# A Mamba and mixture-of-experts block on one core: every engine's order of steps worked out anew, with tables of their own for the first two and the last two slots

## The chip, the core and the metric

The kernel runs on one core of a Trainium2 chip. A core has five instruction queues that run side by side, each strictly in its own order: TensorE (PE), VectorE (DVE), ScalarE (ACT), GpSimd (POOL) and SyncE (SP, which here only issues DMAs). They meet at semaphores alone. The metric is the device time of one launch, in microseconds; the median of the runs is what counts.

## What is computed

The reference is one adaLN block on x of 8 batches x 1024 tokens x 256 channels, float32:

```
h = layernorm(x) * (1 + ca) + sa
x = x + ga * mamba(h)          # rmsnorm, in_proj (512+512), causal conv of 4 taps, silu,
                               # x_proj -> dt, B, C; delta = softplus(...)
                               # s = s * exp(delta * A) + delta * B * u   (16 states x 512 channels, over 1024 tokens)
                               # y = sum over states of s * C, + u * D, * silu(z), out_proj, + h
h = layernorm(x) * (1 + cb) + sb
x = x + gb * ffn(h)            # sigmoid gate, top 4 of 16 experts, each silu(h @ w) * (h @ v) @ out, + a shared expert
```

The six modulation vectors (sa, ca, ga, sb, cb, gb) come from silu(c) @ wmod, one set for each batch.

## The kernel before

The 8192 tokens are cut into 16 chunks of 512. The program is a software pipeline of 18 slots. In slot t three stages run side by side on three chunks: **prepare** of chunk t (norms, in_proj, conv, x_proj, delta, du), **scan** of chunk t-1, and **mix** of chunk t-2 (z gate, out_proj, second norm, router, experts, store). So slot 0 holds only prepare, slot 1 prepare and scan, slots 2 to 15 all three, slot 16 scan and mix, slot 17 mix alone.

Scan is the backbone. A slot has 16 states s and for each 4 channel groups b, 64 groups in all. For each (s, b): POOL makes `scaled` (L713: db_sb = du * B), ACT makes `exp` (L957: da_ps = exp(delta * A)), DVE runs `scan` (L1196, a tensor_tensor_scan over 512 tokens). da_ps has two buffers (NDA = 2), so `exp` number n waits for scan n-2; db_sb has five. When the four scans of a state are done, PE transposes the states into rows_ps (`rows`, L1416, four of them, j = 0 to 3, into two buffers), ACT weighs each with C (`c_scale`, L930) or DVE adds it onto the one before (`c_join`, L1238, states 1, 5, 9, 13; `y_join`, L1247, state 15), and a DMA issued on POOL accumulates it into y_sb (`c_add`, L725). `carry` (L921) keeps the last column for the next chunk.

Mix runs 36 expert units u in a slot, 18 for each half chunk. A unit is `expert_in` (PE, L1480, 24 matmuls into one of three shared PSUM banks), `e_tanh` (ACT, L1023), `e_act` and `e_mul` (DVE, L1296 and L1302; the last frees the bank), `e_weigh` (POOL, L756, with a row that SP loads by `w_load`, L599), and `expert_out` (PE, L1498, 4 matmuls into moe_ps). act has three buffers: `e_tanh` of u waits for `expert_out` of u-3.

Other steps that are named below: `xd`, `xd_t` (PE, L1376, L1383), `dt_high`, `xd_evac` (ACT, L877, L884), `dt_low`, `xd_t_evac` (DVE, L1158, L1164), `dtp` (PE, L1393), `dt_bias` (ACT, L891), `soft_exp` (ACT, L903 and L905), `delta` (DVE, L1170); `x_norm` (ACT, L796), `x_scale`, `x_shift` (DVE, L1122, L1131), `hn_high`, `hn_low` (L823, L1175), `xi` (PE, L1364); at the start of the program `fold` (DVE, L1072 to L1084), `in_low` (DVE, L1054), `mod_rows` (DVE, L1090 to L1105); in slots 1 and 2 `ein_low` (DVE, L1319, nine of them, which split the expert weights).

The order in which each engine takes its steps is not written out by hand. `schedule` gives every step a place in time: a base value from the step lists (`scan_steps`, `prepare_steps`, `mix_steps`, `start_steps`), plus SLOT for each slot, plus a correction by kind of step (SHIFT), by kind and index (PLACE), and for slot 0 (FIRST), slot 17 (LAST) and the program's start (START). Steps are sorted by that value, each engine walks the sorted list and emits the steps that are its own, and the same list gives out the three PSUM banks. The number sets only the order: no engine waits for a time.

## Time and profile before

| | |
|---|---|
| median of 3 runs | 2739.45 us (2736.83 to 2739.89) |
| span of the profiled execution, first to last instruction | 2736.3 us |
| what lies around the span (median less span) | 3.15 us |
| busy: DVE, PE, POOL, ACT | 2398.1, 2351.9, 2256.4, 1945.8 us |
| share of the span: DVE, PE, POOL, ACT | 88%, 86%, 82%, 71% |
| mean granted TensorE clock | 0.943 |

The profiled execution's span and the median are of different executions, 3.15 us apart. Busy shares are means over stages of different kinds; a slot has to be looked at by itself, which is why the rows further down begin with a table by slot. An engine's idle time is listed with what ended it. "x4" in a timeline row is four like instructions in one run. Start and end times are microseconds from the span's start.

### The profile page before, as it was taken

The page shows a single profiled execution, that of the slowest core. Times are in us where ns is not written, and L with a number is a line of the kernel's source. Part 1 is how long each engine was busy: PE and PEld are TensorE (multiplying, and loading weights), DVE is VectorE, ACT ScalarE, POOL GpSimd, SP SyncE. Part 2 cuts the span into 40 slices and gives each one's busy share as a digit, 9 for nine tenths or more (in the row PEclk, how much of TensorE's full clock was granted, in tenths as well). Part 3 has the DMA queues.
Part 4 walks back from the last instruction along what each step waited for, and adds up shares of the span by engine and source line. Part 5 has one row for each costly group of instructions (what it writes and reads, how often), then busy time and mean ns, then how long its engine had stood idle before and what let it go on. Part 6 is the DMA issues. An engine that isn't in the chain of part 4 may idle for free.

```text
span 2736.3 us, 51736 instructions
## 1 busy us (share of the span) xinstructions
PE 2351.9 (86%) x16084; PEld 1889.2 (69%) x16084; DVE 2398.1 (88%) x3815; ACT 1945.8 (71%) x3713; POOL 2256.4 (82%) x2222
## 2 busy tenths in 40 slices
...
GB/s 80 164 143 108 146 148 137 162 115 154 121 145 156 137 161 113 151 130 148 147 132 168 120 145 121 155 156 122 163 114 153 130 159 147 117 156 134 155 70 55
DMA packets 131520, 372.07 MB, mean 136 GB/s; under 512 B 19720, under 2 KB 22408, under 8 KB 130992
## 3 DMA queue, kind: packets, MB, share of 16 engines
...
q8 instruction: 131, 2.15, 0.3%
...
## 4 chain that ended last, share of the span: by engine, by line
POOL 30%; issue 22%; PE 20%; DVE 13%; ACT 7%; DMA 2%; POOLq 1%; DVEq 0%; ACTq 0%; SPq 0%
POOL db_sb L713 16%; PE bank_ps L1480 7%; DVE states L1196 5%; PE moe_ps L1498 5%; POOL act L756 4%; PE rows_ps L1416 4%; POOL y_sb L725 3%; POOL y_sb L734 2%; ACT da_ps L957 2%; PE bank_ps L1376 2%; ACT c_rows L930 1%; POOL du_sb L700 1%; DMA w_sb<-w_dram 1%; DVE act L1296 1%; DVE bank_ps L1143 1%
## 5 line engine op out<-in xcount | busy, mean ns | idle before, releaser
L713 POOL TENSOR_TENSOR db_sb<-du_sb,b_sb 128x512 f32<-128x512 f32 x1024 | 1473.6, 1655 | 32.8 <-DVE states L1196 32.2
L957 ACT ACTIVATE da_ps<-delta,a_sb 128x512 f32<-128x512 f32 x1024 | 696.6, 689 | 170.4 <-DVE states L1196 168.2
L1416 PE MATMUL rows_ps<-ident,states 128*128 128x128 f32 x4096 | 611.4, 287 | 120.9 <-DVE states L1196 85.2
L1480 PE MATMUL bank_ps<-h2T_high,ein_w_high 128*128 128x256 f16 x2304 | 633.9, 275 | 83.8 <-DVE act L1302 50.0
L1196 DVE TENSOR_TENSOR_SCAN states<-da_ps,carry,db_sb 128x512 f32<-128x512 f32 x512 | 644.9, 1273 | 19.0 <-ACT da_ps L957 17.6
L1416 PEld LDWEIGHTS rows_ps<-ident,states 128*128 128x128 f32 x4096 | 503.3, 148 | 210.6 <-DVE states L1196 98.0
L1196 DVE TENSOR_TENSOR_SCAN states<-da_ps,db_sb 128x512 f32<-128x512 f32 x512 | 613.9, 1213 | 34.5 <-ACT da_ps L957 26.3
L1480 PE MATMUL bank_ps<-h2T_low,ein_w_high 128*128 128x256 f16 x2304 | 634.0, 275 | 0.0
L1480 PE MATMUL bank_ps<-h2T_high,ein_w_low 128*128 128x256 f16 x2304 | 633.6, 275 | 0.0
L1498 PE MATMUL moe_ps<-eout_sb,act 128*128 128x256 f32 x2304 | 583.3, 387 | 41.5 <-POOL act L756 40.7
L756 POOL TENSOR_TENSOR act<-act,w_sb 128x256 f32<-128x256 f32 x512 | 472.9, 1115 | 164.0 <-DVE act L1302 141.7
L725 POOL DMA_DIRECT2D y_sb<-c_rows x352 | 379.6, 1078 | 179.1 <-ACT c_rows L930 105.5
L930 ACT ACTIVATE c_rows<-rows_ps,xd_sb 128x512 f32<-128x512 f32 x704 | 467.9, 682 | 70.6 <-PE rows_ps L1416 66.2
L1498 PEld LDWEIGHTS moe_ps<-eout_sb,act 128*128 128x128 f32 x2304 | 408.6, 191 | 113.6 <-POOL act L756 68.8
L1023 ACT ACTIVATE act<-bank_ps 128x256 f32<-128x256 f32 x576 | 218.5, 382 | 286.2 <-PE moe_ps L1498 144.8
L1296 DVE SCALAR_TENSOR_TENSOR act<-act,bank_ps 128x256 f32<-128x256 f32 x576 | 231.6, 407 | 146.0 <-ACT act L1023 145.7
L1480 PEld LDWEIGHTS bank_ps<-h2T_high,ein_w_high 128*128 128x128 f16 x2304 | 226.9, 98 | 127.2 <-DVE act L1302 58.0
L1480 PEld LDWEIGHTS bank_ps<-h2T_high,ein_w_low 128*128 128x128 f16 x2304 | 227.2, 99 | 38.4
L1480 PEld LDWEIGHTS bank_ps<-h2T_low,ein_w_high 128*128 128x128 f16 x2304 | 227.3, 99 | 28.1
L1302 DVE TENSOR_TENSOR act<-act,bank_ps 128x256 f32<-128x256 f32 x576 | 225.2, 410 | 3.3
L1238 DVE SCALAR_TENSOR_TENSOR c_rows<-rows_ps,xd_sb,c_rows 128x512 f32<-128x512 f32 x256 | 181.5, 740 | 3.3 <-PE rows_ps L1416 2.5
L1143 DVE SCALAR_TENSOR_TENSOR bank_ps<-xi_pad,convw_sb,bank_ps 128x512 f32<-128x512 f32 x192 | 143.4, 748 | 5.1 <-ACT bank_ps L858 3.6
...
## 6 DMA issues: line engine op xcount, KB each, us to landing
...
b_sb<-b_dram SPq DMA_DIRECT2D x128, 512.0 KB, 4.8
w_sb<-w_dram SPq DMA_DIRECT2D x256, 256.0 KB, 3.5
...
```

The lines of the kernel that those rows point to most:

```text
L713: pool.tensor_tensor(db_sb[:, n % NDB, :], du_sb[:, slots[t][0][0], b, :], b_sb[:, k % NBPAIR, s % BPAIR, :], ALU.mult).then_inc(sem["scal ...
L725: pool.dma_start(y_sb[:, slots[t][0][0], CPAIR * pair:CPAIR * pair + CPAIR, :], c_rows[:, n % NCR, :, :], accum_op=ALU.add).then_inc(c_add ...
L756: pool.tensor_tensor(place, place, w_sb[:, k % NWROWS, n % WROWS, :], ALU.mult).then_inc(sem["e_weighed"], 1)
L930: ac.activation(c_rows[:, n % NCR, j % CPAIR, :], rows_ps[j % 2][:, :], ACT.Copy, scale=xd_sb[:, slots[t][0][0], j, s:s + 1]).then_inc(sem ...
L957: ac.activation(da_ps[n % NDA][:, :], delta[:, slots[t][0][0], b, :], ACT.Exp, scale=a_sb[:, b, s:s + 1]).then_inc(sem["exp_done"], 1)
L1023: ac.activation(act[:, u % 3, :], bank(key)[:, 0:HALF], ACT.Tanh, scale=0.5 / LIFT).then_inc(sem["e_tanhed"], 1)
L1196: v.tensor_tensor_scan(states[:, n % (2 * NB), :], da_ps[n % NDA][:, :], db_sb[:, n % NDB, :], first, ALU.mult, ALU.add).then_inc(sem["sca ...
L1296: v.scalar_tensor_tensor(place, place, 1.0, bank(key)[:, 0:HALF], ALU.add, ALU.mult).then_inc(sem["e_acted"], 1)
L1302: v.tensor_tensor(place, place, bank(key)[:, HALF:CH], ALU.mult).then_inc(bank_read(key)[0], 1)
L1416: last = pe.transpose(rows_ps[j % 2][:, b * P:b * P + P], states[:, step % 2 * NB + b, j * P:j * P + P], ident[:, :])
L1480: last = pe.matmul(bank(key)[:, a * HALF:a * HALF + HALF], ein_w16[w][:, k, e // 2, at:at + HID], h2T[h][:, k, q * HALF:q * HALF + HALF], ...
L1498: last = pe.matmul(moe_ps[:, n, :], act[:, u % 3, n * P:n * P + P], eout_sb[:, e, :], start=first and n == 0, stop=u % NALL == NALL - 1, s ...
```

## The change

All tables of corrections have new values, and two more tables stand beside FIRST and LAST: SECOND for slot 1 and NEAR_LAST for slot 16. SHIFT and PLACE now also reach the steps of the program's start and the loads of the expert weights (`early_loads`), which had none or other corrections before. Every step that was there is still there, with the same operands, buffers and transfers. Four waits are added, so that `xd_t_evac` may stand later than it did.

```
+def early_loads():
+    out = [(SLOT - 2, ("eout_load",)), (SLOT + 20, ("eout_fold",))]
...
+    ends = {0: FIRST, 1: SECOND, last - 1: NEAR_LAST, last: LAST}
+    listed = [(at - LEAD_P0, START.get(what[0], 0.0), 0.0, 0.0, what) for at, what in start_steps()]
...
-            at = round(at + SLOT * t + SHIFT.get(what[0], 0.0) + PLACE.get(place(what), 0.0) + ends.get(what[0], 0.0), 5)
...
+        listed += [(at + SLOT * t, SHIFT.get(what[0], 0.0), PLACE.get(place(what), 0.0), ends.get(t, {}).get(what[0], 0.0), what) for at, what in mine]
+    latest, keyed = {}, []
+    for n, (at, shift, own, end, what) in enumerate(listed):
+        at = at + shift + own + end
+        latest[what[0]] = max(at, latest.get(what[0], at))
+        keyed.append((latest[what[0]], n, what))
+    order = [what for _, _, what in sorted(keyed)]
...
                         ac.wait_ge(sem["rows_full"], NJ * step + j + 1)
+                        if s == 0 and j == 0:
+                            ac.wait_ge(*bank_read(("xd_t", t - 1)))
...
                     def xd_t_evac(t):
                         key = ("xd_t", t)
+                        if nS(t):
+                            v.wait_ge(*c_scales(NS * nS(t) - 2, NJ - 1))
...
+                        if s == JOINED[0] and j == 0:
+                            v.wait_ge(*bank_read(("xd_t", t - 1)))
...
+                        if not JOINED and j == 0:
+                            v.wait_ge(*bank_read(("xd_t", t - 1)))
```

What the new values come to, sorted: of 3392 steps on DVE 2380 stand at another place in its queue, of 3566 on ACT 2804, of 2690 on PE 1814, of 2099 on POOL 1381, of 523 on SP 309; the mean move is 1 to 2.3 places. The order is the same in each of the slots 2 to 15. Parts of it, with the steps that follow each scan, exp or rows group (s,b or s,j) before and after:

```
                before                                             after
DVE scan 6,2    dt_low, c_join 5.2, 5.3                            c_join 5.2
    scan 6,3    xd_t_evac                                          c_join 5.3, dt_low, e_act 9, e_mul 9
    scan 7,3    e_act 12, e_mul 11, 12                             e_act 12, e_mul 12, e_act 13, e_mul 13
    scan 8,0    e_act 13, e_mul 13                                 -
    scan 8,1    e_act 14                                           xd_t_evac
    scan 8,2    e_mul 14                                           -
    scan 8,3    -                                                  e_act 14, e_mul 14
    scan 12,0   e_act 24, 25, e_mul 24, 25                         -
    scan 12,1   -                                                  e_act 24, e_mul 24
    scan 12,2   e_act 26                                           -
    scan 12,3   e_mul 26                                           e_act 25, 26, e_mul 25
    scan 13,0   e_act 27, 28                                       e_mul 26, e_act 27
    scan 13,1   e_mul 27, 28                                       -
    scan 13,2   -                                                  e_act 28
    scan 13,3   e_act 29, 30, e_mul 29, 30                         e_mul 27, 28
ACT exp 6,3     dt_high, xd_evac                                   carry 5, e_tanh 9      (dt_high after exp 6,2)
    exp 7,0     e_tanh 9, 10                                       xd_evac
    exp 8,1     c_scale 7.0, e_tanh 13, dt_bias 0                  e_tanh 13, dt_bias 0, carry 7, c_scale 7.0, 7.1, dt_bias 1
    exp 8,2     c_scale 7.1, dt_bias 1, 2, e_tanh 14               dt_bias 2
    exp 8,3     c_scale 7.2, dt_bias 3, e_tanh 15, c_scale 7.3     e_tanh 14, c_scale 7.2, dt_bias 3
    exp 9,0     soft_exp 0, carry 8, e_tanh 16                     c_scale 7.3
    exp 9,1     c_scale 8.0                                        e_tanh 15, carry 8, soft_exp 0, e_tanh 16, c_scale 8.0, 8.1
PE  rows 11,3   expert_in 27, 28                                   expert_in 27, expert_out 24
    rows 12,0   expert_out 24, 25                                  -
    rows 12,1   expert_in 29                                       expert_in 28, expert_out 25
```

In all eleven states that ACT weighs, `c_scale` j = 0 and j = 1 now stand in a row ahead of the exp of the next state's group b = 2; before, j = 1 stood behind it. In the program's start, on DVE: before `x_scale 0, x_shift 0, fold, x_scale 1, norm_lift, x_shift 1, mod0_gate, hn_low 0, 1, in_low 0, 1, mod_rows, tap ...`; after `mod0_gate, norm_lift, x_scale 0, x_shift 0, x_scale 1, x_shift 1, in_low 0, 1, fold, hn_low 0, 1, tap ... u 3, mod_rows`. At the start of slot 1 ACT has before `x_norm 0, exp 0,0, x_norm 1`, after `x_norm 0, x_norm 1, exp 0,0`. Slot 1 has its nine `ein_low` at other places among the scans, and `skip_t` moved from states 9 to 11 to states 12 and 13. In slot 17 the engines keep their kinds of steps in the same sequence, with `e_act` and `e_mul` of one unit more often side by side; `z` of j = 0 and 1 on PE stand ahead of rows 14,2.

## Rows read from the trace of the kernel before

**Rows 1.** Busy time by slot: start:end length, each engine's busy us (instructions), granted clock, DMA.

```profile
0.00:79.50 79.50, 31.51 (x84) 12.40 (x84) 36.82 (x79) 41.68 (x81) 23.28 (x34) 0.72 0.33 119
79.50:234.80 155.30, 82.62 (x342) 55.04 (x342) 130.52 (x132) 110.15 (x195) 115.87 (x101) 0.63 0.60 140
234.80:395.70 160.90, 143.76 (x1002) 116.26 (x1003) 149.08 (x238) 119.87 (x225) 139.97 (x139) 0.97 0.59 137
...
716.60:876.20 159.60, 144.03 (x1006) 116.74 (x1006) 145.48 (x237) 120.92 (x237) 140.75 (x139) 0.97 0.60 139
...
2478.20:2616.50 138.30, 124.02 (x898) 105.42 (x895) 123.97 (x191) 86.89 (x158) 119.41 (x118) 0.96 0.62 143
2616.50:2736.30 119.80, 102.03 (x709) 84.36 (x708) 49.08 (x126) 24.61 (x56) 31.93 (x43) 0.96 0.18 53
```

**Rows 2.** Waits of DVE, 486 to 1770 us (eight slots): total us, times, longest.

```profile
DVE act L1296 <- ACT act L1023: 51.5, 60, 1.7
...
DVE dt L1158 <- ACT th_p L884: 8.7, 8, 1.1
```

**Rows 3.** Timeline of DVE, slot 5: start, us, what [idle before <-releaser].

```profile
782.59 0.68 DVE L1158 TENSOR_TENSOR dt<-bank_ps,dt 16x512 f16<-16x512 f32 x1 [1.11 <-ACT th_p L884]
...
795.36 0.42 DVE L1296 SCALAR_TENSOR_TENSOR act<-act,bank_ps 128x256 f32<-128x256 f32 x1 [0.77 <-ACT act L1023]
798.91 0.42 DVE L1296 SCALAR_TENSOR_TENSOR act<-act,bank_ps 128x256 f32<-128x256 f32 x1 [1.54 <-ACT act L1023]
...
804.56 0.42 DVE L1296 SCALAR_TENSOR_TENSOR act<-act,bank_ps 128x256 f32<-128x256 f32 x1 [0.90 <-ACT act L1023]
...
809.82 1.22 DVE L1196 TENSOR_TENSOR_SCAN states<-da_ps,db_sb 128x512 f32<-128x512 f32 x1 [0.92 <-ACT da_ps L957]
...
836.69 0.42 DVE L1296 SCALAR_TENSOR_TENSOR act<-act,bank_ps 128x256 f32<-128x256 f32 x1 [0.60 <-ACT act L1023]
837.98 1.22 DVE L1196 TENSOR_TENSOR_SCAN states<-da_ps,db_sb 128x512 f32<-128x512 f32 x1 [0.87 <-ACT da_ps L957]
...
842.42 0.42 DVE L1296 SCALAR_TENSOR_TENSOR act<-act,bank_ps 128x256 f32<-128x256 f32 x1 [1.23 <-ACT act L1023]
...
849.07 0.42 DVE L1296 SCALAR_TENSOR_TENSOR act<-act,bank_ps 128x256 f32<-128x256 f32 x1 [0.97 <-ACT act L1023]
```

**Rows 4.** Timeline of ACT, slot 5, ahead of three of these waits.

```profile
781.89 0.59 ACT L884 ACTIVATE th_p<-bank_ps 48x512 f32<-48x512 f32 x1
...
797.34 1.27 ACT L891 ACTIVATE delta<-bank_ps,dtb_sb 128x512 f32<-128x512 f32 x2 [0.24 <-PE bank_ps L1393]
798.50 0.38 ACT L1023 ACTIVATE act<-bank_ps 128x256 f32<-128x256 f32 x1
...
842.00 0.38 ACT L1023 ACTIVATE act<-bank_ps 128x256 f32<-128x256 f32 x1 [0.68 <-PE moe_ps L1498]
```

**Rows 5.** Timeline of the start, slots 0 and 1: DVE and PE.

```profile
14.75 0.69 DVE L1131 TENSOR_TENSOR u_sb<-bank_ps,mod_p 128x512 f32<-128x512 f32 x1
...
17.65 0.69 DVE L1122 TENSOR_TENSOR bank_ps<-bank_ps,mod_p 128x512 f32<-128x512 f32 x1
...
29.25 2.47 DVE L1054 SCALAR_TENSOR_TENSOR in_w_low<-states,norm_sb,in_w_high 128x1024 f16<-128x1024 f32 x2
...
31.82 0.59 PE L1364 MATMUL bank_ps<-hnT_high,in_w_high 128*128 128x512 f16 x1 [3.85 <-DVE in_w_low L1054]
...
78.15 0.70 DVE L1122 TENSOR_TENSOR bank_ps<-bank_ps,mod_p 128x512 f32<-128x512 f32 x1 [1.55 <-ACT bank_ps L796]
```

**Rows 6.** Line L1319 (`ein_low`): duration ns min/median/max, first and last start.

```profile
L1319 DVE SCALAR_TENSOR_TENSOR ein_w_low<-zg,ein_w_high x4: 1529/2198/4226, 96.0 to 190.7; 128x1024 f16<-128x1024 f32 x4
```

**Rows 7.** Waits of ACT over the same eight slots.

```profile
ACT c_rows L930 <- PE rows_ps L1416: 33.3, 56, 2.8
```

**Rows 8.** The chain of waits in order of time: start, us, what.

```profile
301.56 2.62 PE bank_ps L1480 x24
```

**Rows 9.** The page's costliest groups: instructions | busy us, mean ns | idle before.

```profile
L957 ACT ACTIVATE da_ps<-delta,a_sb 128x512 f32<-128x512 f32 x1024 | 696.6, 689 | 170.4 <-DVE states L1196 168.2
```

More of the change, by code:

```diff
@@ L238 @@
-FIRST = {"b_store": -4.638, "delta": -2.819, "dt_bias": 2.771, "dt_high": 2.569, "dt_low": 6.847, "dtp": -4.658, "du": 20.092,
-         "ein_high": -18.513, "ein_load": -0.56, "ein_low": 2.016, "h_rms": -0.524, "h_scale": -5.721, "h_square": -2.549,
-         "hn_high": -0.965, "hn_low": -3.241, "hn_t": -7.947, "in_high": 23.347, "in_low": -6.337, "r_add": 5.286, "r_gate": 2.226,
-         "r_store": 3.856, "skip": 5.238, "skip_evac": 9.562, "skip_t": 8.304, "soft_exp": 7.839, "soft_ln": 4.557, "tap": 0.054,
-         "u": 3.728, "u_tanh": 1.139, "x_load": 5.378, "x_norm": -2.74, "x_rstd": -14.374, "x_scale": 3.508, "x_shift": 4.515,
-         "x_stat": -7.043, "xd": 0.786, "xd_evac": -0.005, "xd_t": 13.73, "xd_t_evac": 11.585, "xi": -6.047, "xi_center": -0.781,
-         "xi_copy": -1.708}
@@ L250 @@
-START = {"a_made": -8.949, "constants": -7.533, "ct_silu": -16.404, "ct_tanh": -13.749, "first_loads": 27.458, "fold": 1.055,
-         "in_high": 0.627, "in_low": 7.261, "mod0": 3.212, "mod0_gate": 3.313, "mod0_rows": -4.136, "mod_rows": 0.914, "mod_store": 18.312,
-         "mods": -12.286, "norm_lift": 17.868, "out_scale": 1.297}
+SHIFT = {"b_load": -4.075, "b_store": -0.774, "c_add": 1.548, "c_join": 0.51, "c_scale": 0.671, "carry": 1.751, "delta": -1.404,
+         "dt_bias": 0.716, "dt_high": -1.074, "dt_low": 6.436, "dtp": -1.259, "du": -3.209, "e_act": -0.057, "e_mul": -0.129,
+         "e_tanh": -0.303, "e_weigh": 1.236, "ein_high": -2.54, "ein_load": -8.035, "ein_low": 3.444, "eout_fold": 7.161,
+         "eout_load": -39.417, "exp": 1.131, "expert_in": -0.101, "expert_out": 0.782, "h2_high": 0.138, "h2_low": -0.01, "h2_scale": 0.42,
+         "h2_t": -2.304, "h_rms": -4.436, "h_scale": -3.293, "h_square": 0.94, "hn_high": -0.686, "hn_low": 0.906, "hn_t": 3.499,
+         "logit": -1.011, "logit_exp": 2.301, "mod_m_load": -7.536, "mod_p_load": -51.943, "op": 1.293, "op_gate": 1.514, "out_add": 1.84,
+         "out_gate": 0.676, "out_store": 3.191, "r_add": 11.77, "r_gate": 1.021, "r_load": 12.711, "r_store": -3.854, "router": 3.104,
+         "rows": 0.174, "scaled": 1.14, "scan": 0.004, "skip": -0.464, "skip_evac": 4.69, "skip_t": -1.302, "soft_exp": -3.082,
+         "soft_ln": 1.864, "tap": 0.19, "u": -0.176, "u_tanh": 0.428, "w_evac": -1.906, "w_load": -0.429, "w_store": 7.456, "w_t": -3.769,
+         "x1": 1.091, "x1_norm": -4.802, "x1_rstd": -5.323, "x1_stat": 1.485, "x_load": -7.339, "x_norm": 0.681, "x_rstd": 5.697,
+         "x_scale": -0.157, "x_shift": -0.7, "x_stat": -1.105, "xd": -4.991, "xd_evac": 3.144, "xd_t": 6.368, "xd_t_evac": 8.145,
+         "xi": -1.404, "xi_center": -0.012, "xi_copy": -0.284, "y_evac": -1.028, "y_gate": -0.757, "y_join": 0.428, "y_t": -0.212,
+         "z": -5.131, "z_gate": -0.023, "z_tanh": -2.943}
```

85 lines of the change are left out of this document (44 added, 41 removed), and 144 rows, old and new, of the table PLACE.

## The prediction

> **What bounds the kernel now.** I read the table of busy time by slot first [rows 1]. Slots 2 to 15 are alike: 160.2 us each on average (234.8 to 2478.2 is 14 slots), of which DVE is busy 145.5 to 149.1, PE 143.8 to 144.0, POOL 140.0 to 140.8 and ACT 119.9 to 120.9. So the kernel is bound by DVE with PE and POOL close behind, and yet some 13 us of each such slot are DVE's idle time. No engine can go below its busy time by a change of order, and all operations are kept; the idle time is the whole of what the change can win, 14 x 13 = 182 us at the very most in those slots. The two ends are looser: slot 0 has 36.8 us of DVE in 79.5, slot 1 has 130.5 in 155.3, slot 16 124.0 (and PE 124.0) in 138.3, slot 17 102.0 of PE in 119.8.
>
> Second, who ends DVE's idle time: in eight slots, 51.5 us before `e_act` waiting for `e_tanh`, 8.7 us before `dt_low` waiting for `xd_evac` [rows 2]; the reader is to see that ACT ends it, though ACT is the least busy of the four. Third, where in the slot: the timeline of slot 5 [rows 3]. The waits come in three places, the same in every slot. Place A, states 6: 1.11 us before `dt_low`. Place B, states 8 and 9: 0.77 (`e_act` 13), 1.54 (`e_act` 14), 0.90 (`e_act` 15), 0.92 (a scan), 4.1 us. Place C, states 12 and 13: 0.60, 0.87, 1.23, 0.97, 3.7 us. Together 8.9 of the 13 us. Between them DVE runs nearly without a gap.
>
> **Part 1, the inner slots.** Place A: `xd_evac` runs at 781.89 and ends at 782.48, and `dt_low` starts at 782.59 [rows 3, 4], because ACT reaches it only after the two `dt_high` while DVE has nothing between scan 6,2 and `dt_low` to fill the time. After, DVE puts `c_join` 5.2, scan 6,3 and `c_join` 5.3 in between, 1.22 for the scan and about 0.69 for each `c_join`, as for the other 512-column steps of DVE, 2.6 us of work [rows 3, 5]; ACT has an exp, an `e_tanh` and one more exp in there, 0.69 + 0.38 + 0.69 = 1.8 us [rows 4, 9]. The wait goes: 1.1 us. Place B: `e_tanh` 14 starts at 798.50 behind `c_scale` and two `dt_bias` that alone take 797.34 to 798.61 [rows 4]; DVE wants it one scan after `e_act` 13. After, `e_act` 14 stands behind scan 8,3, two scans later (2.4 us against a wait of 1.54), so that wait goes. But `e_act` 13 now stands right behind scan 7,3, while its `e_tanh` still follows an exp that needs that scan: I keep some 0.6 of its 0.77. And the two `soft_exp` (two ACT instructions over 1024 columns each; an estimate of 2.1 us from exp's 0.69 for 512 columns) still sit among exps in state 9; going through ACT's queue from scan 7,3 to scan 10,0 I find 0.6 + 0.4 + 0.7 + 0.7 + 0.5 = 2.9 us of waits where 4.1 were. Gain 1.2. Place C: `e_tanh` 27 starts at 842.00 when PE ends `expert_out` 24 [rows 4], which stands on PE behind `expert_in` 28, a run of 2.62 us [rows 8]. After, `expert_out` 24 stands ahead of `expert_in` 28, so it comes up to 2.62 us sooner, and on DVE `e_act` 28 has two scans more to wait. The 0.60 + 1.23 + 0.97 (2.8 us) of `e_act` waits should shrink to next to nothing; the scan's 0.87 I leave.
>
> Sum: 1.1 + 1.2 + 2.8 = 5.1 us a slot, if nothing is given back. Something will be: PE and POOL have only 16 and 20 us of idle time a slot [rows 1], and every wait that goes on DVE pulls the next scan, and with it rows, `c_scale` and `c_add`, forward into engines that are as full. I take half, 2.6 us a slot; the bounds are 0 (all given back) and 5.1. 14 slots x 2.6 = 36 us.
>
> **Part 2, the four waits.** `xd_t_evac` now waits for the `c_scale` of state 14 of the slot before, which was over seven states ago; `c_scale` 0.0 and `c_join` 1.0 wait for an `xd_t_evac` of the slot before, half a slot ago. Behind each are queued the rest of ACT's or DVE's steps, but all three are fulfilled when they are reached. The fourth is never emitted. Some three waits a slot that are met at once: between 0 and 0.1 us each, an estimate from `dt_low`'s start 0.11 after the end of what it waits for [rows 3, 4]; 3 x 16 x 0.1, 5 us in all at most. I take 0.
>
> **Part 3, slot 0.** Before, DVE does `fold` between `x_shift` 0 (ends 15.44) and `x_scale` 1 (starts 17.65) [rows 5]; the first thing that waits for `x_shift` 1 is the squaring on ACT. After, `fold` stands behind `in_low`: 17.65 - 15.44 = 2.2 us sooner, of which I take 2.0, since `x_norm` 1 has to be there. Then `in_low`, 2.47 us at 29.25, is the last that `xi` on PE waits for (31.82) [rows 5]. After, it stands ahead of `hn_low`, in a stretch where DVE waits anyway: 2.4 us more. `mod_rows` moves off the path too, into the wait for dt. At the start of slot 1 `x_norm` 1 no longer stands behind a table load and an exp; its `x_scale` starts at 78.15 after a wait of 1.55 [rows 5], of which 1.4 go, for the first exp then comes last. Sum 5.8 us; 3 to 7. SP's big expert load is put ahead of the loads of x and B there; I take it as hidden behind `du` and `x_rstd` on POOL, and let the bounds of this part stand for up to 3 us if it is not.
>
> **Part 4, slot 1, slot 16 and the tail.** Slot 1 has 24.8 us of DVE idle time and TensorE at 0.63 of its clock, near the lower of its two levels (1.2 GHz) [rows 1]; the order there is so different that I can't follow it step by step. Its nine `ein_low` are the same instruction and last between 1.5 and 4.2 us in the four that one row shows [rows 6], so what they cost depends on when they come. With a least duration of 1.5 and a median of 2.2, nine of them carry some 6 us that another order could win or double: bounds -6 to +6 for the slot, I take a gain of 2. The Trainium skill (SBUF — State Buffer, "SBUF: two separate sides") has a rule for this: VectorE and GpSimd share one port pair, and a VectorE instruction with two SBUF inputs and a GpSimd instruction that reads SBUF shut each other out for a whole instruction. The spread of the row agrees; by that rule `ein_low` ought to stand where POOL is idle, and the new order gives no sign that it does, so by the page the gain of slot 1 would be 0 and the sum 2 us smaller. For slot 16 and 17 I take 2 us: PE, which carries the tail, is idle 14.3 + 17.8 us there [rows 1], most of it in the one chain from y to the router weights, whose steps have the same sequence as before. Bounds 0 and 8.
>
> **Sum.** 36 + 5.8 + 2 + 2 = 46 us. The profiled execution has a span of 2736.3 and the median is 3.15 more; taken off the median, 2739.45 - 46 = 2693.
>
> **The rivals.** (1) *Given back in full* (0.13): the inner slots are set by a ring of DVE, ACT, PE and POOL and a wait that goes comes back elsewhere; only the start is won. 2739.45 - 5.8 - 2 = 2731. For it: three engines are within 7 us of one another [rows 1]. Against it: the waits are DVE's own, and DVE is the fullest. (2) *More than half* (0.15): nothing is given back, and slot 1 and the tail give more. 14 x 5.1 + 7 + 6 + 8 = 92, so 2647, or 2660 where a little is lost. (3) *Slower: the paired c_scale* (0.15). In eleven states `c_scale` j = 1 now stands ahead of the exp that scan b = 2 waits for. ACT stands still there if PE has not yet done rows j = 1. ACT already waits for rows 56 times in eight slots, 4.2 us a slot, the longest 2.8 [rows 7], about one `expert_in` of 2.62 [rows 8] that PE can't break off. If PE reaches rows j = 1 a further 0.6 us after ACT does in each of eleven states, 6.6 us a slot, DVE has only two scans (2.4 us) and what stands beside them to cover an exp, two `c_scale` and an exp (four of 0.69, of which some 0.6 each in a row, 2.5 us) [rows 3, 9], so all of it shows on the scans: 14 x (6.6 - 5.1) = 21 us, less 6 at the start: 2755. It decides from 0.46 us on (11 x 0.46 = 5.1). Against it: PE's own list now has rows j = 0 and 1 side by side. (4) *The new order does nothing at all* (0.05): where waits only trade places, 2737 to 2745.
>
> **How the numbers follow.** Forecast 2693 (0.52), by itself 2672 to 2716: 14 x 1.1 to 14 x 4.1 for the inner slots with the ends as they are. The range has to leave out no more than 0.2: 2652 to 2743 leaves out most of rival 3 and the farthest of rival 2. A measurement of this kernel tells 0.2% (5.5 us) from no change, so faster is below 2734. Faster: 0.52 + 0.15 + 0.09 of rival 1 = 0.76; same: 0.04 of rival 1, 0.04 of rival 4 and 0.01 of rival 3, 0.09; slower 0.15.
>
> **What would show it.** Place A right: no wait of DVE L1158 for ACT L884. Place B: the wait of L1296 before `e_act` 14 gone, one of about 0.6 before `e_act` 13. Place C: `expert_out` 24 ahead of `expert_in` 28 and DVE's wait for ACT L1023 in states 12 and 13 under 1 us. Start: the first scan at about 74 us where it was 79.5. Slots 2 to 15: 157.8 us each. Rival 3 would show as more than 33.3 us of ACT L930 waiting for PE L1416 and scans waiting for exp at b = 2. I am wrong if the waits at A, B and C go and the slot is as long as before, or if new ones of a kind not seen before stand elsewhere.

## The result, and the profile after

| | before | after |
|---|---|---|
| median | 2739.27 us (2736.83 to 2739.89) | 2641.75 us (2636.48 to 2643.97) |
| span of the profiled execution | 2736.3 us | 2640.4 us |
| busy DVE, PE, POOL, ACT | 2398.1, 2351.9, 2256.4, 1945.8 us | 2409.0, 2337.5, 2245.4, 1927.8 us |

The ratio is 0.9644 (95% interval 0.963 to 0.9657), 97.5 us less. I had forecast 46 us less, and a range whose low end was 2652. The direction was right and the size was less than half of what came. The time is near that of my rival 2, in which nothing is given back: 2647.

The lines below are those of the changed kernel. Its line numbers are 20 to 28 higher: `scaled` L733, `c_add` L745, `e_weigh` L776, `c_scale` L952, `exp` L979, `e_tanh` L1045, `dt_low` L1180, `xd_t_evac` L1188, `scan` L1220, `y_join` L1275, `e_act` L1324, `e_mul` L1330, `ein_low` L1347, `rows` L1444, `expert_in` L1508, `expert_out` L1526. First busy time by slot, the view of [rows 1]; the stretches run from the first scan of a slot to that of the next. After the length of a stretch stand the busy us of PE, of PE's weight loads, of DVE, ACT and POOL, then the granted clock, the DMA share and GB/s.

```profile
0.00:76.40 76.40, 34.68 (x84) 12.69 (x84) 40.94 (x79) 40.43 (x77) 23.93 (x33) 0.72 0.34 124
76.40:220.70 144.30, 82.01 (x348) 57.16 (x348) 131.37 (x133) 110.58 (x197) 114.45 (x102) 0.66 0.66 151
220.70:374.90 154.20, 142.05 (x1006) 115.95 (x1004) 149.11 (x238) 118.88 (x226) 139.94 (x139) 0.98 0.61 143
...
685.40:837.70 152.30, 141.16 (x1007) 116.35 (x1005) 145.68 (x237) 119.67 (x238) 139.94 (x139) 0.98 0.63 145
...
2389.00:2525.50 136.50, 123.41 (x899) 104.92 (x898) 125.27 (x190) 84.55 (x156) 120.79 (x120) 0.95 0.64 145
2525.50:2640.40 114.90, 99.82 (x702) 83.32 (x700) 49.81 (x124) 24.60 (x56) 31.33 (x42) 0.95 0.19 56
```

Against [rows 1]: slots 2 to 15 take 2389.0 - 220.7 = 2168.3 us, 154.9 each where they took 160.2 (75 us in all). Slot 1 takes 11.0 less, the start 3.1, slot 16 1.8 and slot 17 4.9. VectorE's busy time in slots 2 to 15 is nearly what it was (147.3 us a slot on average, 147.0 before), and so is the granted clock, 0.98 against 0.97; what went is idle time, 13.3 us a slot before and 7.6 after. Who ends VectorE's idle time over eight slots, 529.7 to 1767.8 us, is the view of [rows 2]. Its second row in the kernel before, 486 to 1770 us, was

```profile
DVE states L1196 <- ACT da_ps L957: 20.6, 44, 0.9
```

and in the changed kernel the view begins with

```profile
DVE act L1324 <- ACT act L1045: 25.3, 38, 3.0
DVE y_sb L1275 <- DMA y_sb<-c_rows: 7.0, 8, 1.5
DVE states L1220 <- ACT da_ps L979: 4.7, 14, 0.7
```

The 51.5 us before `e_act` are 25.3, the 20.6 of scans waiting for `exp` are 4.7, the 8.7 before `dt_low` have no row any more, and one wait of size is new: `y_join` (state 15) waits for the last accumulating DMA of GpSimd, 0.9 us a slot. Where they stand, in the timeline of VectorE in slot 5, the view of [rows 3]:

```profile
751.28 0.68 DVE L1180 TENSOR_TENSOR dt<-bank_ps,dt 16x512 f16<-16x512 f32 x1
...
760.04 0.42 DVE L1324 SCALAR_TENSOR_TENSOR act<-act,bank_ps 128x256 f32<-128x256 f32 x1 [0.29 <-ACT act L1045]
...
770.30 0.42 DVE L1324 SCALAR_TENSOR_TENSOR act<-act,bank_ps 128x256 f32<-128x256 f32 x1 [0.39 <-ACT act L1045]
...
772.42 0.42 DVE L1324 SCALAR_TENSOR_TENSOR act<-act,bank_ps 128x256 f32<-128x256 f32 x1 [1.24 <-ACT act L1045]
...
799.53 2.34 DVE L1220 TENSOR_TENSOR_SCAN states<-da_ps,db_sb 128x512 f32<-128x512 f32 x2 [0.67 <-ACT da_ps L979]
...
829.55 1.41 DVE L1275 SCALAR_TENSOR_TENSOR y_sb<-rows_ps,xd_sb,y_sb 128x512 f32<-128x512 f32 x2 [1.19 <-DMA y_sb<-c_rows]
```

Place A has no wait left (751.28). Of place B 0.29 is left before `e_act` 13 and 0.39 + 1.24 before `e_act` 16 and 17 in state 9. Of place C no wait of `e_act` is left, but a scan's 0.67 (799.53), and another scan waits 0.38 us at 806.14.

### The profile page after: what moved, and what is told of

Read it like the earlier page. It is cut to its first block, busy times and chain, and to the rows that moved or that the text cites. A ratio compares the mean times of both kernels' runs of the same rounds, so it can differ in the third digit from the quotient of the medians.

```text
span 2640.4 us, 51751 instructions
## 1 busy us (share of the span) xinstructions
PE 2337.5 (89%) x16084; PEld 1887.7 (71%) x16084; DVE 2409.0 (91%) x3815; ACT 1927.8 (73%) x3713; POOL 2245.4 (85%) x2222
## 4 chain that ended last, share of the span: by engine, by line
POOL 31%; issue 27%; PE 13%; DVE 12%; DMA 8%; ACT 6%; POOLq 1%; DVEq 0%; ACTq 0%; SPq 0%
POOL db_sb L733 18%; DMA y_sb<-c_rows 6%; PE bank_ps L1508 5%; POOL act L776 5%; POOL y_sb L745 5%; DVE states L1220 4%; PE moe_ps L1526 4%; PE rows_ps L1444 2%; DMA w_sb<-w_dram 1%; ACT da_ps L979 1%; ACT c_rows L952 1%; DVE zg L1233 1%; DVE bn L1252 1%; DVE x L1246 1%; ACT act L1045 1%
## 5 line engine op out<-in xcount | busy, mean ns | idle before, releaser
L733 POOL TENSOR_TENSOR db_sb<-du_sb,b_sb 128x512 f32<-128x512 f32 x1024 | 1401.4, 1452 | 91.8 <-DVE states L1220 91.6
L979 ACT ACTIVATE da_ps<-delta,a_sb 128x512 f32<-128x512 f32 x1024 | 704.0, 691 | 130.4 <-DVE states L1220 124.9
L1444 PE MATMUL rows_ps<-ident,states 128*128 128x128 f32 x4096 | 597.4, 288 | 105.3 <-DVE states L1220 81.6
L1508 PE MATMUL bank_ps<-h2T_high,ein_w_high 128*128 128x256 f16 x2304 | 633.4, 275 | 46.0 <-DVE act L1330 22.8
L1220 DVE TENSOR_TENSOR_SCAN states<-da_ps,carry,db_sb 128x512 f32<-128x512 f32 x512 | 641.7, 1275 | 9.4 <-ACT da_ps L979 7.2
L1444 PEld LDWEIGHTS rows_ps<-ident,states 128*128 128x128 f32 x4096 | 503.7, 149 | 190.3 <-DVE states L1220 93.2
L1508 PE MATMUL bank_ps<-h2T_low,ein_w_high 128*128 128x256 f16 x2304 | 633.2, 275 | 0.0
L1508 PE MATMUL bank_ps<-h2T_high,ein_w_low 128*128 128x256 f16 x2304 | 633.2, 275 | 0.0
L1220 DVE TENSOR_TENSOR_SCAN states<-da_ps,db_sb 128x512 f32<-128x512 f32 x512 | 610.5, 1214 | 13.6 <-ACT da_ps L979 13.0
L776 POOL TENSOR_TENSOR act<-act,w_sb 128x256 f32<-128x256 f32 x512 | 472.1, 1000 | 146.8 <-DVE act L1330 122.0
L1526 PE MATMUL moe_ps<-eout_sb,act 128*128 128x256 f32 x2304 | 579.2, 382 | 11.7 <-POOL act L776 10.5
L952 ACT ACTIVATE c_rows<-rows_ps,xd_sb 128x512 f32<-128x512 f32 x704 | 462.2, 685 | 77.6 <-PE rows_ps L1444 56.4
L1526 PEld LDWEIGHTS moe_ps<-eout_sb,act 128*128 128x128 f32 x2304 | 403.2, 190 | 64.4 <-POOL act L776 20.7
L745 POOL DMA_DIRECT2D y_sb<-c_rows x352 | 380.4, 1081 | 61.6 <-DMA y_sb<-c_rows 28.8
L1045 ACT ACTIVATE act<-bank_ps 128x256 f32<-128x256 f32 x576 | 215.3, 380 | 176.3 <-PE moe_ps L1526 128.6
L1324 DVE SCALAR_TENSOR_TENSOR act<-act,bank_ps 128x256 f32<-128x256 f32 x576 | 231.8, 410 | 92.7 <-ACT act L1045 91.4
L1508 PEld LDWEIGHTS bank_ps<-h2T_high,ein_w_high 128*128 128x128 f16 x2304 | 227.1, 99 | 90.5 <-DVE act L1330 28.7
L1508 PEld LDWEIGHTS bank_ps<-h2T_high,ein_w_low 128*128 128x128 f16 x2304 | 227.1, 99 | 43.7 <-issue 0.5
L1508 PEld LDWEIGHTS bank_ps<-h2T_low,ein_w_high 128*128 128x128 f16 x2304 | 227.3, 99 | 27.8
L1330 DVE TENSOR_TENSOR act<-act,bank_ps 128x256 f32<-128x256 f32 x576 | 234.8, 417 | 10.1
```

The source lines that it names most:

```text
L733: pool.tensor_tensor(db_sb[:, n % NDB, :], du_sb[:, slots[t][0][0], b, :], b_sb[:, k % NBPAIR, s % BPAIR, :], ALU.mult).then_inc(sem["scal ...
L745: pool.dma_start(y_sb[:, slots[t][0][0], CPAIR * pair:CPAIR * pair + CPAIR, :], c_rows[:, n % NCR, :, :], accum_op=ALU.add).then_inc(c_add ...
L776: pool.tensor_tensor(place, place, w_sb[:, k % NWROWS, n % WROWS, :], ALU.mult).then_inc(sem["e_weighed"], 1)
L952: ac.activation(c_rows[:, n % NCR, j % CPAIR, :], rows_ps[j % 2][:, :], ACT.Copy, scale=xd_sb[:, slots[t][0][0], j, s:s + 1]).then_inc(sem ...
L979: ac.activation(da_ps[n % NDA][:, :], delta[:, slots[t][0][0], b, :], ACT.Exp, scale=a_sb[:, b, s:s + 1]).then_inc(sem["exp_done"], 1)
L1045: ac.activation(act[:, u % 3, :], bank(key)[:, 0:HALF], ACT.Tanh, scale=0.5 / LIFT).then_inc(sem["e_tanhed"], 1)
```

## The experiments

Every kernel below is the changed program, its four waits included, and gives each step its number either from the new tables (`new`) or from those of before (`old`), or takes single steps out of the list and puts them right behind another one (`move`). The code is shortened to the condition or the moved steps. The computation is whole in all of them. Times are medians; beside them stands the kernel before on the same chip, which took 2738.4 to 2740.1 in all.

**1. The inner slots alone, and the three places one by one.**

```
inner_new   key = (new if 2 <= t <= 15 else old)
place_a     key = old; in slots 2 to 15:
+           move(("c_join", t, 5, 3), behind=("scan", t, 6, 3))
+           move(("dt_low", t), behind=("c_join", t, 5, 3))
place_b     key = old; in slots 2 to 15:
+           move(("e_act", t, 14), behind=("scan", t, 8, 3))
+           move(("e_mul", t, 14), behind=("e_act", t, 14))
place_c     key = old; in slots 2 to 15:
+           move(("expert_out", t, 24), behind=("expert_in", t, 27))
```

> Only the steps of slots 2 to 15 take their places from the new tables; the start and slots 0, 1, 16 and 17 keep the order of before. W (nothing is given back in the inner slots): the slots are as short as in the changed kernel, 14 x 5.4 = 75 us off, 2664 us. H (half is given back, as in the prediction, and the rest of the 97 us came in through the ends, which leave the rings in another phase): 14 x 2.6 = 36 off, 2703. A value of 2664 +- 5 speaks for W, 2695 and more for H.

Measured: 2658.41 against 2739.39, 81 us less (ratio 0.970, 0.9685 to 0.9714). So by the values set before the run nothing is given back in the inner slots when all of their order is new, and they don't need the ends for it: in its profile slots 2 to 15 take 2163.0 us.

> The order of before, where in slots 2 to 15 VectorE takes c_join 5.3 and dt_low behind scan 6,3 and not ahead of it. This takes away the 1.1 us wait at place A and nothing else. W: all of it stays, 14 x 1.1 = 15 us off, 2724. H: half, 2731. R (given back in full): 2739. The wait of dt_low for ACT L884 of before is gone from the rows in any case.

Measured: 2739.24 against 2739.39 (ratio 1.000, 0.999 to 1.001). All of it is given back. The rows say where most of it went; VectorE in slot 5 of place_a, where L1313 is `dt_low` and L1321 `xd_t_evac`:

```profile
783.97 0.68 DVE L1313 TENSOR_TENSOR dt<-bank_ps,dt 16x512 f16<-16x512 f32 x1
785.50 0.23 DVE L1321 COPY xd_sb<-bank_ps 128x64 f32<-128x64 f32 x1 [0.85 <-PE bank_ps L1544]
```

`dt_low` waits for nothing now. Two steps on, `xd_t_evac` waits 0.85 us for TensorE's `xd_t`, which VectorE had reached later before. The same run shows that the four added waits cost nothing that can be measured.

> The order of before, where in slots 2 to 15 VectorE takes e_act 14 and e_mul 14 behind scan 8,3 (before: behind scan 8,1 and 8,2). The wait of 1.5 us before e_act 14 goes. W: 14 x 1.5 = 21 us off, 2718. H: 2729. R: it comes back at e_act 15, which waits for an e_tanh on the same full ACT: 2737 to 2741.

Measured: 2748.11 against 2739.39 (1.003, 1.0019 to 1.0042), 8.7 us slower, outside all three expectations. Over the eight slots the wait that was aimed at did shrink, and the scans' waits for `exp` grew by more (L1457 is `e_act`, L1353 `scan`; before 51.5 and 20.6):

```profile
DVE act L1457 <- ACT act L1178: 42.1, 59, 1.4
DVE states L1353 <- ACT da_ps L1112: 33.2, 59, 1.0
```

Which step on ScalarE makes the scans later no run here shows.

> The order of before, where in slots 2 to 15 TensorE takes expert_out 24 ahead of expert_in 28, one step on one queue. e_tanh 27 comes up to 2.6 us sooner, and the waits of e_act 27 in state 13 (1.2 and more, in the profile 2.1 us a slot over the group behind scan 13,0) should go. W: 14 x 2.1 = 29 us off, 2710. H: 2725. R: 2739, with the wait moved to e_act 28 or to a scan.

Measured: 2765.19 against 2739.39 (1.0098, 1.0083 to 1.0113), 25.8 us slower: this too fits none of them. All engines at the place, in slot 5 of place_c (L908 is `e_weigh`, L1658 `expert_out`, L1576 `rows`, L1084 `c_scale`, L1456 `e_act`):

```profile
845.86 3.28 POOL L908 TENSOR_TENSOR act<-act,w_sb 128x256 f32<-128x256 f32 x3
...
847.84 1.13 PE L1658 MATMUL moe_ps<-eout_sb,act 128*128 128x256 f32 x4 [1.91 <-POOL act L908]
...
850.12 0.60 PE L1576 MATMUL rows_ps<-ident,states 128*128 128x128 f32 x4
...
850.76 0.69 ACT L1084 ACTIVATE c_rows<-rows_ps,xd_sb 128x512 f32<-128x512 f32 x1 [3.26 <-PE rows_ps L1576]
...
851.75 0.77 DVE L1456 SCALAR_TENSOR_TENSOR act<-act,bank_ps 128x256 f32<-128x256 f32 x2 [3.48 <-ACT act L1177]
```

The same stretch of the kernel before:

```profile
838.79 3.29 POOL L756 TENSOR_TENSOR act<-act,w_sb 128x256 f32<-128x256 f32 x3
...
840.77 1.99 PE L1498 MATMUL moe_ps<-eout_sb,act 128*128 128x256 f32 x8 [0.17 <-POOL act L756]
```

Before, TensorE came to `expert_out` 24 just when GpSimd had weighed its unit: it waited 0.17 us. That `expert_in` 28 stood ahead of it was not what made it late, it filled the wait. Put ahead, TensorE stands still 1.91 us, and `expert_in` 28 and behind it the `rows` group start only after that. ScalarE, whose order is the old one, stands 3.26 us at the `c_scale` of these rows, with `e_tanh` behind it, and VectorE waits 3.48 for that `e_tanh`. Over the eight slots ScalarE's waits for rows rise from 33.3 to 61.2 us and VectorE's before `e_act` from 51.5 to 66.0; the latter, 1.8 us a slot, is the 25.8 us of the run.

**2. Parts of the slot, all five queues.** The old place is the number of before, less SLOT times the slot; 4 units are a state.

```
w2          key = (new if 2 <= t <= 15 and 24 <= old place < 44 else old)
w3          key = (new if 2 <= t <= 15 and not 0 <= old place < 44 else old)
w23         key = (new if 2 <= t <= 15 and not 0 <= old place < 24 else old)
w3_old_act  as w3, but the steps of ScalarE keep old
```

> In slots 2 to 15 the steps of all five queues whose old place lies in states 6 to 10 (places A and B) take their new places; the rest of the slot and the ends stay as before. J (a wait is won where the queues around it are moved together, and then stays won): VectorE's idle time behind these scans is 6.0 us a slot in the trace of before and 2.8 in that of after, so 14 x 3.0 = 42 off, 2697. R (only the whole order works; a part gives nothing, as the single steps did): 2735 or more. Half-way, 2718, would mean that half is given back.

Measured: 2795.13 against 2740.08 (1.0199, 1.0184 to 1.0214), 55 us slower.

> The same for the steps whose old place lies in states 11 to 15 and at the border of the slot (place C). Idle time there 6.4 us a slot before and 2.3 after. J: 14 x 4.1 = 57 off, 2682. R: 2735 or more. Half: 2710.

Measured: 2783.62 against 2740.08 (1.0159, 1.0144 to 1.0174), 44 us slower.

> Both parts at once; states 0 to 5 keep the order of before. J: the two gains add, and since all inner slots new gave 81 us, the sum is some 81 to 99 off, 2640 to 2660; states 0 to 5 bring nothing by themselves. R: well above 2680, since the slot is not whole. If the gains of the two parts run apart from their sum by over 20 us, the ring is what counts and not the places.

Measured: 2759.94 against 2740.08 (1.0078, 1.0061 to 1.0094), 20 us slower.

> As w3, but ScalarE keeps the order of before in these states; TensorE, VectorE, GpSimd and SyncE are new. The lone step on TensorE at place C cost 26 us. If what it lacked was VectorE's part (e_act 28 two scans later), this gives most of w3's gain, within 15 us of it. If ScalarE's own order is needed, since e_tanh 25 to 31 and the paired c_scale stand elsewhere, it is over 2720.

Measured: 2832.53 against 2740.08 (1.0339, 1.0324 to 1.0354), 92 us slower, 49 more than w3. ScalarE's part is needed. In VectorE's timeline of w2 (slot 5) new waits stand at the cut into state 6, and place C, whose order is that of before, waits longer than before (L1454 is `e_act`, L1305 `u`):

```profile
788.16 0.69 DVE L1305 SCALAR_TENSOR_TENSOR u_sb<-th_p,bank_ps 128x512 f32<-128x512 f32 x1 [0.82 <-ACT th_p L1017]
789.65 0.75 DVE L1454 SCALAR_TENSOR_TENSOR act<-act,bank_ps 128x256 f32<-128x256 f32 x2 [0.80 <-ACT act L1175]
...
857.65 0.42 DVE L1454 SCALAR_TENSOR_TENSOR act<-act,bank_ps 128x256 f32<-128x256 f32 x1 [2.11 <-ACT act L1175]
```

**3. The same with the cuts where the two orders agree.** At 24 and 44 there are 12 and 18 steps that one order has behind it and the other ahead; at 7.25 and 39.25 only 3 and 4.

```
x2          key = (new if 2 <= t <= 15 and 7.25 <= old place < 39.25 else old)
x3          key = (new if 2 <= t <= 15 and not 7.25 <= old place < 39.25 else old)
x3_sp       as x3, and the steps of SyncE new in the whole of slots 2 to 15
```

> As the run of states 6 to 10, but cut where the two orders have nearly the same steps behind them: in slots 2 to 15 the steps with an old place of 7.25 to 39.25 are new (states 2 to 9, places A and B). At the old cuts of 24 and 44, 12 and 18 steps stand on different sides in the two orders, at these 3 and 4. S (the parts keep their gain, and what the first cuts lost was lost at their seams): idle time behind these scans goes from 5.6 to 3.8 us, 14 x 1.8 = 25 off, 2714. R (only the whole order works): slower than 2739 again.

Measured: 2726.05 against 2739.72 (0.9951, 0.9936 to 0.9966), 13.7 us faster, half of the 25.

> The rest: in slots 2 to 15 the steps with an old place from 39.25 on and up to 7.25 of the next slot are new (states 10 to 15, the border, states 0 and 1; place C). S: 6.5 us of idle time become 2.4, 14 x 4.1 = 57 off, 2682; the two parts add to the 81 us of all inner slots within 10. R: slower than 2739, and the sum of the two is far from 81.

Measured: 2795.93 against 2739.72 (1.0208, 1.0193 to 1.0223), 56 us slower. GpSimd's costliest wait in x3 from 486 to 1770 us (total, times, longest), and SyncE's issues (L733 is `b_load`, L739 `w_store`):

```profile
POOL db_sb L863 <- DMA b_sb<-b_dram: 91.9, 7, 13.5
```

```profile
892.97 0.38 SPq L733 DMA_DIRECT2D b_sb<-b_dram  x1
932.97 0.33 SPq L739 DMA_DIRECT2D w_dram<-wT  x1
933.39 0.85 SPq L733 DMA_DIRECT2D b_sb<-b_dram  x2
```

At the cut `w_store` had come to stand ahead of two `b_load` on SyncE. It waits for the router's weights until 932.97, and two loads of the rows of B, which GpSimd needs for `scaled`, are issued behind it.

> As the run of states 10 to 1 (which took 2796), but SyncE has its new order in the whole of slots 2 to 15. In that run GpSimd waited 91.9 us in eight slots for the transfer of the B rows, because at the cut w_store stands ahead of b_load 2 on SyncE and waits for a w_evac that is new and later. If that one step is the seam's price, the part now shows its own gain: S, 14 x 4.1 = 57 off, 2682, and 57 + 14 is near the 81 of all inner slots. If it stays above 2739, the loss is in the ring of the other queues.

Measured: 2702.38 against 2738.43 (0.9867, 0.9852 to 0.9882), 36 us faster, and GpSimd's waits over the same stretch have no row for the B rows any more. SyncE's order alone is worth 93 us between these two kernels. The two parts give 13.7 + 36 = 50 us, the whole 81.

**4. One queue left behind, and single steps inside the new order.**

```
in_old_pool key = (new if 2 <= t <= 15 and the step isn't GpSimd's else old)
c_split     key = new; slots 1 to 16: move(("c_scale", t, s, 1), behind=("exp", t, s + 1, 2))
undo_c      key = new; slots 2 to 15: move(("expert_out", t, 24), behind=("expert_in", t, 28))
soft_late   key = new; slots 2 to 15: e_act 17, e_mul 17 behind scan 9,2
+           move(("soft_exp", t, 0), behind=("e_tanh", t, 17))
```

> Slots 2 to 15 new on TensorE, VectorE, ScalarE and SyncE, but GpSimd keeps its order of before; the ends as before. All five new took 2658. If the gain needs all queues in step: far slower, 2700 or more (e_weigh and c_add then stand at places that the others have left). If GpSimd's order is a detail: 2658 to 2670.

Measured: 2911.67 against 2738.43 (1.0639, 1.0617 to 1.066): 173 us slower than before and 253 slower than with GpSimd's steps new as well. Its waits from 486 to 1770 us begin with

```profile
POOL y_sb L878 <- ACT c_rows L1085: 85.6, 26, 9.6
```

so GpSimd stands at `c_add` for a `c_scale` that ScalarE now makes later, and `scaled` and `e_weigh` stand behind it.

> The changed kernel, where c_scale j = 1 stands behind the exp of group 2 of the next state again, as before, in all eleven states and the slots 1 to 16. Rival 3 (the pair costs): faster than 2642, by up to 11 x 0.6 x 14 = 92 us at its full price. If the pair is free: 2642 within 5. If the pair is a part of the gain (rows' bank is free sooner, so TensorE does not wait at j = 3): slower than 2650.

Measured: 2652.7 against 2738.43 (0.9688, 0.967 to 0.9705), 11 us slower than the changed kernel. The pair that I feared is part of the gain.

> The changed kernel with one TensorE step of slots 2 to 15 put back: expert_out 24 behind expert_in 28, the very edit whose opposite cost 26 us in the kernel before. If a step's worth is its own: 26 us faster, 2616. If its worth depends on what stands around it, as part of the new order it earns: expert_out 24 would then wait for rows and expert_in (about 2.6 us later), e_tanh 27 with it, 14 x 0.5 to 14 x 2.6, 2649 to 2678.

Measured: 2654.84 against 2739.54 (0.969, 0.9676 to 0.9704), 13 us slower than the changed kernel, with a wait at `e_act` in state 13 of slot 5 (L1456) that the changed kernel doesn't have:

```profile
812.89 0.42 DVE L1456 SCALAR_TENSOR_TENSOR act<-act,bank_ps 128x256 f32<-128x256 f32 x1 [1.69 <-ACT act L1177]
```

To have `expert_out` 24 ahead of `expert_in` 28 costs 26 us in the old order and earns 13 in the new one. The two edits are not exact opposites: in the old order the step goes ahead of `expert_in` 28 and `rows` 12,0, here it falls behind `rows` 12,1 as well.

> The changed kernel, aimed at its longest remaining wait (2.1 us a slot before e_act 16 and 17, in state 9): soft_exp 0 (2.1 us on ScalarE) goes behind e_tanh 17, and e_act 17 with e_mul 17 behind scan 9,2. If a wait that is seen in the trace can be won by moving the steps that stand in it: 14 x 1 to 14 x 2.1, 2612 to 2628. If, as with the single steps in the kernel before, it only moves, since ScalarE works without a gap over the whole of state 9: 2640 to 2655.

Measured: 2668.55 against 2739.54 (0.9741, 0.9724 to 0.9757), 27 us slower than the changed kernel. From 486 to 1770 us the waits for `e_tanh` fell, and those of the scans for `exp` rose by more; the changed kernel and then soft_late:

```profile
DVE act L1324 <- ACT act L1045: 26.2, 39, 3.0
...
DVE states L1220 <- ACT da_ps L979: 5.7, 16, 0.7
```

```profile
DVE states L1354 <- ACT da_ps L1113: 30.7, 33, 3.4
DVE act L1458 <- ACT act L1179: 16.2, 34, 1.1
```

**5. The ends.**

```
slot1_old   key = (old if t == 1 else new)
start_old   key = (old for the start, slot 0 and the early weight loads, else new)
early_old   key = (old for eout_load, eout_fold, ein_load, ein_high, ein_low, else new)
```

> The changed kernel, slot 1 in the order of before. If the 11.1 us of slot 1 are won by its own order (four waits of ein_low for ein_high and two of hn_low that are gone): 2642 + 11 = 2653. If they are won by what stands around it (the big expert load put ahead in slot 0): within 3 us of 2642.

Measured: 2643.95 (0.9652, 0.9637 to 0.9666): 2.2 us slower than the changed kernel, within its spread.

> The changed kernel, the start, slot 0 and the early weight loads in the order of before (kinds in slot 1 on stay new). By the trace the first scan comes 3.1 us sooner in the new one: 2642 + 3 = 2645. If the early load is what shortens slot 1 too: up to 2656.

Measured: 2656.22 (0.969, 0.9674 to 0.9706): 14.5 us slower than the changed kernel.

> The changed kernel with only the early weight loads (eout_load, ein_load, ein_high, ein_low, eout_fold) in the order of before. The run with start, slot 0 and these all old took 14.5 us more than the changed kernel, that with slot 1 old 2.2 more. If the 11 us of slot 1 lie in the places of ein_high and ein_low: 2642 + 11 = 2653. If they lie in the start: 2645.

Measured: 2650.64 (0.9678, 0.9663 to 0.9692): 8.9 us slower than the changed kernel. The nine `ein_low` in slot 1 (busy us, mean ns), in the kernel before, in the changed one, and in early_old, where they are L1477:

```profile
L1319 DVE SCALAR_TENSOR_TENSOR ein_w_low<-x,ein_w_high 128x1024 f16<-128x1024 f32 x5 | 12.9, 2578 | 0.1
L1319 DVE SCALAR_TENSOR_TENSOR ein_w_low<-zg,ein_w_high 128x1024 f16<-128x1024 f32 x4 | 10.2, 2538 | 4.8 <-ACT ein_w_high L1028 4.8
```

```profile
L1347 DVE SCALAR_TENSOR_TENSOR ein_w_low<-x,ein_w_high 128x1024 f16<-128x1024 f32 x5 | 16.4, 3285 | 0.0
L1347 DVE SCALAR_TENSOR_TENSOR ein_w_low<-zg,ein_w_high 128x1024 f16<-128x1024 f32 x4 | 8.1, 2033 | 0.0
```

```profile
L1477 DVE SCALAR_TENSOR_TENSOR ein_w_low<-zg,ein_w_high 128x1024 f16<-128x1024 f32 x4 | 17.1, 4266 | 0.0
L1477 DVE SCALAR_TENSOR_TENSOR ein_w_low<-x,ein_w_high 128x1024 f16<-128x1024 f32 x5 | 16.3, 3251 | 1.1 <-ACT ein_w_high L1180 1.0
```

They take 23.1 us before, 24.5 after and 33.4 in early_old. In its profile slot 1 lasts 156.9 us, 12.6 more than in the changed kernel: 8.8 of them VectorE is busy, as much as the nine instructions are longer, and 3.9 it is idle. In slot1_old slot 1 lasts 149.9. But slots 2 to 15 are shorter than in the changed kernel's profile in both, by 6.2 and by 4.8 us, and the two executions as a whole are only 5.3 and 1.1 us longer. That the run and the nine instructions both differ by 8.9 us is chance. What makes the later slots shorter no run shows; the changed kernel's own executions lie between 2636.5 and 2644.0.

## Why the prediction was right and where it failed

**What bounds the kernel: held.** VectorE's mean busy time in an inner slot stayed within 0.3 us, its idle time went from 13.3 to 7.6 us, and all that was won in the inner slots lay in that difference.

**Part 1, the step that failed: "I take half".** The sum of the waits, 5.1 us a slot, was near what the slot gained: 5.3 in the changed kernel, 5.8 (81 / 14) with only the inner slots new. The factor of one half was mis-sized; it measured 1. That is 39 of the 51.5 us by which the forecast missed; slot 1 brought 9 more than I took, slot 16 and the tail 5, and the start 3 less. I put it in because PE and POOL have little idle time. The in-between kernels show that such giving back is real, but that it isn't a share of each wait. A single step moved in the old order gives back all (A), or more than all (B ends 8.7 us slower, C 25.8). With every queue moved together, the sum comes in whole. The range had both ends, 0 and 5.1 a slot, and I should have seen that the change was of the second kind: it moves 1381 to 2804 steps on each of the four busy engines.

That 5.1 met 5.3 so closely is partly luck. I called VectorE nearly without a gap outside the waits that I listed, but slot 5 has six more of 0.16 to 0.59 us around B and C, 2.1 us together, and over eight slots the scans waited 20.6 us for `exp`, of which 4.7 are left: 2.0 us a slot that I had mostly not counted. Against them stand new waits that I had not foreseen, `y_join`'s 0.9 us a slot the largest, and `e_act`, whose waits fell by 3.3 us a slot where my sums of B and C took 4.

By place: A gave its 1.1 us as predicted, by the rows. At B 2.9 us were to stay; in slot 5 0.29 + 0.39 + 1.24 = 1.9 did, and 0.24 before `xd_t_evac` and 0.19 before a scan beside them. At C I forecast that a scan's 0.87 stays; two scans' 0.67 and 0.38 did, and the waits of `e_act` went. So the places were read right. The mechanism at C was not: I took TensorE's own queue (`expert_in` 28 ahead of `expert_out` 24) for the cause, and place_c shows that GpSimd's `e_weigh` was 0.17 us behind it as the next limit, and that ScalarE's `c_scale` waits for the rows that then come late. In the order in which all queues are new it is worth 13 us (undo_c).

**Part 2, the waits: held.** Every kernel of the experiments carries them; place_a, whose only other edit moves one wait to the next step, takes what the kernel before takes, and no row of it or of the changed kernel shows a wait at `c_scale` or `c_join` for an `xd_t_evac`.

**Part 3, the start: 3.1 where I took 5.8.** The rows of the changed kernel:

```profile
17.52 2.36 POOL L711 TENSOR_TENSOR conv<-u_sb,mod_p 128x1024 f32<-128x1024 f32 x1 [5.25 <-ACT conv L828]
...
18.45 3.70 DVE L1076 SCALAR_TENSOR_TENSOR in_w_low<-states,norm_sb,in_w_high 128x1024 f16<-128x1024 f32 x2 [2.30 <-ACT in_w_high L801]
...
22.64 3.02 DVE L1102 TENSOR_SCALAR dtw<-db_sb 16x512 f16<-16x512 f32 x2
...
25.69 1.41 DVE L1104 SCALAR_TENSOR_TENSOR dtw<-db_sb,dtw 16x512 f16<-16x512 f32 x1
...
26.06 0.60 ACT L843 ACTIVATE hnT_high<-bank_ps 128x512 f16<-128x512 f32 x1 [0.79 <-PE bank_ps L1381]
...
28.78 0.59 PE L1392 MATMUL bank_ps<-hnT_high,in_w_high 128*128 128x512 f16 x1 [1.90 <-DVE hnT_low L1199]
```

`in_low` did go ahead and `xi` starts at 28.78 instead of 31.82, 3.0 sooner and not 4.4. Two things took the rest. The first is GpSimd's order, which I had not looked at: a product for the residual (L711) stands ahead of the norm's scale now, the scale is ready at 23.11 where it was 21.83, and `hn_high` starts at 26.06 instead of 27.16, 1.1 sooner where I took 2.0. The second is a price that I took as fixed: the moved instructions lie beside GpSimd's work now, `in_low` takes 3.70 instead of 2.47, and three instructions of `fold` 3.02 for two and 1.41 (before 0.86 and 0.68 in the same view), so that `hn_low` starts at 27.24, 0.6 after the first `hn_high` is done. Of the 3.0, 1.8 are left at the first scan. What `x_norm` 1 gives there, 1.3, was forecast as 1.4.

**Part 4, slot 1: 11 us where I took 2.** I took the gain from how long `ein_low` lasts (and read only four of the nine; the other five lasted 1.20 to 4.16 us before). The nine did not become shorter (23.1 and 24.5 us). What went is idle time, 24.8 to 12.9 us, the 4.8 us of `ein_low` waiting for `ein_high` among it. The bounds of -6 to +6 came from durations alone, though [rows 1] showed 24.8 us of idle time; they should have reached to 12 and more. early_old shows that with the early loads at their old places all of slot 1's gain is gone (156.9 us, 155.3 before), slot1_old that with its other steps in the old order half of it is gone (149.9). In the whole run the first is worth 8.9 us and the second 2.2, which is within the spread. The Trainium skill (SBUF — State Buffer, "SBUF: two separate sides") says that a VectorE instruction with two SBUF inputs and a GpSimd instruction that reads SBUF shut each other out. The traces agree in that VectorE's instruction takes longer beside GpSimd's: in the changed kernel the `ein_low` at 152.87 us, with no GpSimd instruction beside it, takes 1.20 us, and the one at 111.05, beside two `scaled`, 4.34; in early_old one takes 6.17 beside a run of `scaled`:

```profile
157.56 5.88 POOL L863 TENSOR_TENSOR db_sb<-du_sb,b_sb 128x512 f32<-128x512 f32 x4
158.36 6.17 DVE L1477 SCALAR_TENSOR_TENSOR ein_w_low<-zg,ein_w_high 128x1024 f16<-128x1024 f32 x1
```

That each shuts the other out for a whole instruction the durations alone don't show.

**Slot 16 and the tail: 1.8 + 4.9 where I took 2.** In inner_new, with the ends of before, the tail takes 119.8 us; with the new ones 114.9. In the chain from y to the router little moved: VectorE's wait for `h2T_high` is 7.4 us where it was 7.5. That `e_act` and `e_mul` side by side release the banks sooner is argued from the order, not tested.

**The rivals.** (1), given back in full, is what the single step at A does, and not what the change does. (2) came true in its sum; its ends were divided otherwise (7, 6 and 8 us for the start, slot 1 and the tail, where 3.1, 11.0 and 6.7 came). (3), the pair of `c_scale`, is refuted: ScalarE waits 56.4 us for rows in the whole run where it waited 66.2, and without the pair the kernel is 11 us slower. (4) is out.

**Slips in the sums.** Slots 2 to 15 at 160.2 - 2.6 would be 157.6 us each and not 157.8, and the upper end of the forecast by itself, 2739.45 - 14 x 1.1 - 9.8, is 2714 and not 2716. Neither changes what is said above.

**What stays open.** The two parts with good cuts sum to 50 of 81 us. How much of the other 31 was lost at the cuts and how much only the whole can give, the runs don't tell. x2 should have given 25 by its idle times and gave 13.7. Why a gain in slot 1 is partly lost again in slots 2 to 15, and which step at place B makes the scans wait, is open too.
